# Attention and mixture of experts on one core: bias rows on TensorE, ScalarE bringing the projections out, router products a quarter into a tile, and one deviation ahead of two placings

## The reference

```
x = x + gnn(layernorm(x), adj)
x = x + ffn(layernorm(x))

gnn(n, adj):  h = n @ W.T + b_W
              e = leaky((h @ a1)[:, None] + (h @ a2)[None, :] + b_a)    # slope 0.2
              e = where(adj > 0, e, -9e15)
              return softmax(e, axis=1) @ h
ffn(n):       logits = n @ Wr + br;  the 2 best of 64 experts, gates = softmax of the 2
              out = sum over the 2 of gate * (relu(n @ W1[e] + b1[e]) @ W2[e] + b2[e])
```

## Time and profile before

| what | value |
|---|---|
| median of three runs | 280.89 us (279.63 to 281.43) |
| profiled execution, whole | 280.6 us |
| profiled execution, span | 278.9 us |
| mean granted TensorE clock | 0.918 |
| busy PE / DVE / ACT / POOL | 222.4 / 218.6 / 172.0 / 166.4 us |

### The profile page before, as it was taken

How to read it: one execution, slowest core, us unless ns; L and a number is a source line. 1 busy time by engine, 2 the same in 40 slices (tenths; PEclk the granted TensorE clock), 3 DMA queues, 4 the chain that set the end, 5 groups by cost and what they waited for, 6 DMA issues and landing times.

```text
span 278.9 us, 6179 instructions
## 1 busy us (share of the span) xinstructions
PE 222.4 (80%) x1849; PEld 212.8 (76%) x1849; DVE 218.6 (78%) x629; ACT 172.0 (62%) x386; POOL 166.4 (60%) x194
## 2 busy tenths in 40 slices
PE   1493399898968796886985368999999999999840
PEld 1372399798968696786984357999999999999740
DVE  4857989998999989999958733889887766766464
ACT  2743668797666585765751506878877777777400
POOL 5850011634478848888875755444888888866600
PEclk9999579999979999997998556999999999999995
DMA  6993454488474950810991113223148710100067
GB/s 162 227 199 71 79 94 79 82 211 209 139 185 89 285 179 12 292 32 19 374 418 49 59 43 91 66 57 80 42 133 321 256 41 31 40 28 24 31 199 262
DMA packets 11119, 36.88 MB, mean 132 GB/s; under 512 B 2256, under 2 KB 2832, under 8 KB 10320
## 3 DMA queue, kind: packets, MB, share of 16 engines
q0 software_dynamic: 5232, 14.98, 24.6%
q1 hardware_dynamic: 5424, 21.11, 21.6%
q10 hardware_dynamic: 432, 0.40, 0.5%
HBM read 39.36 MB, written 5.51 MB: 161 GB/s over the span
## 4 chain that ended last, share of the span: by engine, by line
PE 49%; DVE 27%; issue 9%; DMA 7%; POOL 5%; ACT 1%; SPq 1%; POOLq 0%; DVEq 0%; ACTq 0%
PE bank L1090 16%; PE bank L1102 15%; DVE arena L693 8%; PE bank L988 6%; DVE arena L699 4%; PE bank L972 4%; POOL table L419 2%; DVE arena L684 2%; DMA arena<-result 2%; DMA xs<-in_x 2%; PE bank L938 2%; DVE xs L705 2%; PE bank L1079 1%; PE bank L948 1%; DVE st L708 1%
## 5 line engine op out<-in xcount | busy, mean ns | idle before, releaser
L988 PE MATMUL bank<-arena 128*128 128x130 f32 x512 | 62.7, 279 | 1.4 <-ACT arena L542 1.3
L988 PEld LDWEIGHTS bank<-arena 128*128 128x128 f32 x512 | 60.3, 194 | 2.1 <-DVE xs L705 1.5
L1090 PE MATMUL bank<-arena 128*128 x384 | 60.4, 281 | 0.1
L1102 PE MATMUL bank<-w2s,arena 128*128 x384 | 58.8, 276 | 0.2 <-issue 0.2
L419 POOL DMA_INDIRECT table<-rows_in,pos x32 | 47.9, 1496 | 11.9 <-issue 8.1
L1090 PEld LDWEIGHTS bank<-arena 128*128 128x128 f32 x384 | 51.2, 194 | 0.5 <-issue 0.2
L1102 PEld LDWEIGHTS bank<-w2s,arena 128*128 128x128 f32 x384 | 50.6, 192 | 0.6 <-issue 0.6
L972 PE MATMUL bank<-ident,arena 128*128 128x128 f32 x256 | 35.5, 299 | 19.0 <-DVE arena L699 19.0
L868 DVE SCALAR_TENSOR_TENSOR arena<-bank,arena 128x128 f32 x96 | 33.6, 350 | 21.7 <-PE bank L1102 20.6
L972 PEld LDWEIGHTS bank<-ident,arena 128*128 128x128 f32 x256 | 32.5, 156 | 20.1 <-DVE arena L699 20.1
L601 ACT ACTIVATE arena<-bank,arena 128x128 f32<-128x128 f32 x96 | 35.1, 366 | 18.1 <-PE bank L1090 16.9
(11 more groups left out here) (190 smaller groups left out, 274.1 us busy)
## 6 DMA issues: line engine op xcount, KB each, us to landing
arena<-in_adj POOLq DMA_DIRECT2D x16, 512.0 KB, 5.4
w2s<-in_w SPq DMA_DIRECT2D x8, 768.0 KB, 4.6
arena<-in_w SPq DMA_DIRECT2D x6, 1024.0 KB, 9.2
arena<-in_w SPq DMA_DIRECT2D x4, 512.0 KB, 4.9
w2s<-in_w SPq DMA_DIRECT2D x4, 512.0 KB, 3.8
xs<-in_x SPq DMA_DIRECT2D x4, 256.0 KB, 6.3
arena<-result SPq DMA_DIRECT2D x2, 512.0 KB, 4.3
arena<-result SPq DMA_DIRECT2D x4, 256.0 KB, 6.1
```

The source lines that it names most:

```text
L988: ins = pe.matmul(OB[t % 2][:, 0:D + 2], pt_r[:, t % 2, j, :], h[:, j, :], start=(j == 0), stop=(j == T - 1))
L1090: ins = pe.matmul(hp(p, b), w1u[:, p % UW, P * b:P * b + P], xT_all[:, bass.ds(column, P)], start=True, stop=True)
L1102: ins = pe.matmul(yp(p), hT[:, p % UH, b, :], w2s[:, bass.ds(u, 1), b, :].rearrange("p e d -> p (e d)"), start=(b == 0), stop=(b == HB - 1))
```

## The change

On PE, the four quarters of the score row now come with only the turns of the quarters between them, and all projections behind them. Each projection is followed by a matmul of one row (a row of ones times the bias row `hbias`) into the same PSUM columns, which adds the bias. `xhT` lies in the second buffer of `pt_r`. The projections are brought out by ACT: two pairs of tiles and a quarter of s8 ahead of its scores of tile 0, the other six pairs and the rest of s8 ahead of its scores of tile 1. DVE, in place of ACT, writes the normalised rows of tiles 12 to 15; it sets eight small constants ahead of the statistics and no longer behind the projections. POOL loads blocks 2 and 3 of adj behind all four chunks of statistics. In attend, `route_b` stands behind 4 of the 16 products and no longer behind 8. At the end of attention, POOL makes the deviation of tiles 12 and 13 ahead of the two placings of tile 9, and DVE does place of group 3 ahead of the residual of tile 14.

```diff
-    PLACED = [..., (1, 7, 14), (2, 8, 15), (2, 9, 15)]
+    PLACED = [..., (1, 7, 14), (2, 8, 15)]
...
 # GpSimd
-                if c < 3:
-                    load(c + 1)
+                if c == 0:
+                    load(1)
+            load(2)
+            load(3)
...
             rstd_of(6)
+            place(2, 9)
             rstd_of(7)
...
 # ScalarE
             scale(2)
-            scale(3)
...
+            def h_evac(c):
+                act.wait_ge(s_h, c + 1)
+                act.activation(h[:, 2 * c:2 * c + 2, 0:D + 1],
+                               bank[4 + c % 4][:, 0:2 * (D + 1)].rearrange("p (t d) -> p t d", t=2), ACT.Copy).then_inc(s_hs, 1)
+
+            def slope(t0, t1):
+                act.wait_ge(s_hs, t1 // 2)
+                act.activation(s8[:, t0:t1], h[:, t0:t1, D], ACT.Copy, scale=1.0 - SLOPE).then_inc(s_s8, 1)
+
+            h_evac(0)
+            h_evac(1)
+            slope(0, 4)
+
             def scores(t):
-                if t == 0:
-                    act.wait_ge(s_s8, 1)
+                if t == 1:
+                    for c in range(2, 8):
+                        h_evac(c)
+                    slope(4, T)
+                if t in (0, 4):
+                    act.wait_ge(s_s8, 1 + t // 4)
...
 # VectorE
             xT_evac(0)
+            penalty(0)
+            dve.wait_ge(s_nm, 4)
+            for t in range(12, T):
+                ins = dve.tensor_scalar(xh[:, t, :], xs[:, t, :], rstd[:, t:t + 1], nm2[:, t:t + 1], ALU.mult, ALU.add)
+            ins.then_inc(s_norm3, 1)
             xT_evac(1)
-            penalty(0)
             xT_evac(2)
-            dve.wait_ge(s_was, 1)
-            h_evac(0)
-            h_evac(1)
             penalty(1)
-            for c in range(2, 6):
-                h_evac(c)
             scores(0)
-            h_evac(6)
-            h_evac(7)
-            dve.wait_ge(s_hs, 8)
-            dve.tensor_scalar(s8[:, :], h[:, :, D], 1.0 - SLOPE, None, ALU.mult).then_inc(s_s8, 1)
...
             leaky(T - 1)
+            place(3)
             residual(T - 2)
-            place(3)
             top2(4)
...
 # TensorE
-                        ins = pe.matmul(bank[4 + c % 4][:, j * (D + 1):(j + 1) * (D + 1)], xhT[:, P * t:P * t + P],
-                                        wt_s[:, :], start=True, stop=True)
+                        at = bank[4 + c % 4][:, j * (D + 1):(j + 1) * (D + 1)]
+                        pe.matmul(at, xhT[:, P * t:P * t + P], wt_s[:, :], start=True, stop=False)
+                        ins = pe.matmul(at, ones_f[0:1, :], hbias[0:1, :], start=False, stop=True)
...
-                        if j == T // 2 and t == LAST[q] + 2:
+                        if j == T // 4 and t == LAST[q] + 2:
                             route_b(q)
```

More of the change, by code:

```diff
@@ L25, in build @@
     LAST = [START[q + 1] - 1 for q in range(NG)]
-    PLACED = [(0, 0, 8), (0, 1, 9), (0, 2, 10), (0, 3, 11), (1, 4, 12), (1, 5, 13), (1, 6, 13), (1, 7, 14), (2, 8, 15), (2, 9, 15)]
+    PLACED = [(0, 0, 8), (0, 1, 9), (0, 2, 10), (0, 3, 11), (1, 4, 12), (1, 5, 13), (1, 6, 13), (1, 7, 14), (2, 8, 15)]
     LNS = [(t, t + 2) for t in range(0, T - 2, 2)] + [(T - 2, T - 1), (T - 1, T)]
@@ L102, in build @@
         zl = xT_all[:, 0:TOPK * T * D].rearrange("p (k t d) -> p k t d", k=TOPK, t=T)
-        xh, xhT = z_r[:, 1, :].rearrange("p (t d) -> p t d", t=T), z_r[:, 2, :]
+        xh, xhT = z_r[:, 1, :].rearrange("p (t d) -> p t d", t=T), pt_r[:, 1, :, :].rearrange("p t i -> p (t i)")
         s8 = sb("s8", [P, T])
@@ L207, in build @@
         s_norm = sem("s_norm")
+        s_norm3 = sem("s_norm3")
         s_xT = sem("s_xT")
@@ L650, in stats @@
                 dve.tensor_scalar(ve[:, 4 * c:4 * c + 4], mv[:, 4 * c:4 * c + 4, 1], EPS, None, ALU.add).then_inc(s_stat, 1)
[L652 to L658, removed]
             def xT_evac(b):
@@ L676, in _ @@
             dve.memset(padrow[:, :, :], 0.0).then_inc(s_set, 1)
+            dve.wait_ge(s_pool, 4)
+            dve.wait_ge(s_set, 1)
+            dve.tensor_scalar(sidx[0:P // 2, :], pidx[0:P // 2, :], 2.0, None, ALU.mult)
+            dve.tensor_scalar(sidx[P // 2:P, :], pidx[P // 2:P, :], 2.0, 1.0 - P, ALU.mult, ALU.add)
+            for into in (r_lo, r_hi, r_blk):
+                dve.tensor_copy(into[E:E + 1, :], iota_p[E:E + 1, 0:TAB])
+            for k in range(1 + TOPK):
+                ins = dve.tensor_scalar(padrow[:, k, ID_COL:ID_COL + 1], pidx[:, :], float(DUMP + (E + (k - 1) * P if k else 0)), None, ALU.add)
+            ins.then_inc(s_rows, 1)
             for c in range(4):
@@ L924, in turn_x @@
             def turn_x(b):
-                pe.wait_ge(s_norm, b + 1)
+                if b < 3:
+                    pe.wait_ge(s_norm, b + 1)
+                else:
+                    pe.wait_ge(s_norm3, 1)
                 for c in range(CB):
@@ L954, in _ @@
             pe.wait_ge(s_was, 1)
-            for b in range(4):
[L956 to L961, removed]
+            scores_row(0)
+            turn_x(2)
+            scores_row(1)
+            turn_x(3)
+            scores_row(2)
+            scores_row(3)
+            pe.wait_ge(s_set, 1)
+            for b in range(4):
+                project(b)
             def turn(t):
@@ L1033, in _ @@
             route_a(5)
+            route_c(4)
             route_b(5)
-            route_c(4)
             route_a(6)
```

## The result

The changed kernel takes **285.56 us** (median of four runs, 284.63 to 286.12) against 281.16 for the kernel before, 1.015 times as long (95% interval 1.009 to 1.022). The forecast was 273.4 us with a range up to 277.3: wrong in sign. (The kernel before, timed again beside the experiments, had medians of 279.9 to 280.6 us.) The profiled execution takes 286.12 us with a span of 284.3, 5.4 us more than the span before, of which the experts' stage behind the first fetch of rows makes 1.4 (115.3 us against 113.9; it lies between 113.9 and 115.6 in all runs here, also in the fastest). The other 4.0 us are 6.5 lost at the start, less 1.6 and 0.9 won behind it.

A forecast was written before the change was run, and what follows sets the result against it. The prediction took PE's chain to bound the start, DVE attention and POOL the placings behind it. Start 4.6, router 1.6 and placings 1.3 sum to 7.5 us: 280.9 - 7.5 = 273.4 us, range 271.8 to 277.3.

The forecast's parts named there:

- part three: ACT and PE at the start: each projection takes 0.22 us, its bias matmul another 0.22.
- rival (a): Projections at the start: bias matmuls don't overlap, about 0.16 us more per change of tile, 277.8 us; chance 0.11.
- the slower case (c): Projections at the start: changes of tile cost 0.27 us each, kernel slower than before at 282.0 us; chance 0.03.
- the bounds of the start: Start's gain of 4.6 us: 5.0 without DVE's wait, 3.9 if PE's clock falls while waiting 2 us for ACT.
- The start, part one: Twelve projections leave PE's stretch ahead of the last score-row quarter: first z at 20.6, gain 2.6 us.
- Part two: DVE's list at the start loses 1.74 us of work and a 0.69 us wait; leaky(2) could begin at 36.9.
- ScalarE's part: ACT brings out the projections at the start; DVE waits 0.4 to 0.5 us for low(1).
- Router: Router's products in attention come 0.9 us sooner, ending DVE's 0.79 us waits in groups 0 and 1: 1.6 us.
- Placings: POOL at the end of attention: the first of the eight last placings begins at 150.5, not 151.85, 1.3 us gained.
- The stretched deviation: POOL's deviation of tiles 12 and 13, beside DVE's leaky, takes 2.75 us instead of 0.73.
- Sum: Whole kernel: 4.6 + 1.6 + 1.3 = 7.5 us gained, median 273.4 us.

The follow-up runs named there:

- full height: The changed kernel with its 16 bias matmuls on tiles of 128 rows (identity times replicated bias rows): 274.36 us, 0.976 of the kernel before.
- the run with 64 rows: The changed kernel with bias matmuls on tiles of 64 rows (1/64 in each, times equal bias rows): 280.02 us in one run.
- the two runs with four changes: The changed kernel with four 258-column bias matmuls in a row ahead of eight projections: 278.23 us with one-row tiles, 276.2 with 128 rows.

## Why the prediction was wrong

**The step that failed** is in part three: "its bias matmul streams the same 129 columns, so I take another 0.22", with its rival (a) put at 0.11 and the slower case (c) at 0.03. The columns were right (0.22 in full height). The change of tile was 0.19 us each, 0.16 in (a); and what neither rival had is that the clock level falls under it. Together each change came to (20.2 - 7.1) / 32 = 0.41 us, above the 0.33 from which (c) made the kernel slower by over 1%; by (c)'s sum 0.41 gives 280.9 + 13.1 - 7.5 = 286.5 us, and 285.6 was measured. The only term for a falling clock was 0.7 us, in the bounds of the start, for a wait of 2 us; the fall cost 5.5. The place of (c) was right; its price for a change was reached only with the clock's share, about half of it, which (c) didn't name; and its chance was too small.

**Why I gave it so little.** I set the trace against the rule of the Trainium skill (TensorEngine Tiling (Array Packing), Key Properties) with one pair of merged rows, 64*1 and then 65*128, and read no gap between them. A merged row of eight hides its own spacing, and the ends of matmuls in it are modelled. The single records say otherwise. Timeline of PE of the kernel before, a window that holds the last four of the eight:

```profile
162.32 0.36 PE L1061 MATMUL bank<-r_slot,radix 64*1 64x24 f32 x4
162.61 0.53 PE L1066 MATMUL bank<-r_lo,side 65*128 65x96 f32 x1
```

Four records of 0.2 us each within 0.36 stand some 0.05 apart, so the last begins near 162.48, and L1066 0.13 later. A gap was there to be seen, though about 0.1 us long where the granted clock is 0.50, less than the 0.28 us that the same level shows further down; these matmuls have 24 columns, and the row couldn't have given the price. What the runs show agrees with the rule: each change of mode costs a pause, 0.19 us here. That it is the engine draining is the page's word for it; the rows show the distance between starts only.

**The start, part one:** the mechanism right; that it came out better, 3.7 us in place of 2.6 (3.2 in the run of full height), is luck as far as the traces show. PE comes up to its full pace at the start at another moment in each trace, though the code up to there is nearly the same. In the changed kernel's trace:

```profile
12.97 1.91 PE L947 MATMUL bank<-arena,x2T 128*128 128x512 f32 x2
...
15.53 1.03 PE L947 MATMUL bank<-arena,x2T 128*128 128x512 f32 x2
```

Here the pace had doubled by 15.5, where I had it stay at 18; over the twelve traces with this start it did so between 15.0 and 18.1, and the first z began between 19.27 and 20.72. The last of these is the run with 64 rows, where it doubled at 18: 0.1 us from the forecast's 20.6. That this is the clock level is taken from the pace alone; the column of the granted clock reads 1.00 from 12 to 20 us in both kernels, at the half pace too. **Part two:** right, shown with full height: third leaky at 36.97 against my 37.4, and 16.85 us behind the first z against my 16.8. **ScalarE's part:** right in the run of full height (0.50 us wait). **Router:** 1.6 forecast, 1.6 in the trace, 1.8 in the medians. **Placings:** 1.3 forecast, 0.9 in one trace and 0.8 between two, nothing in the medians; the idle 1.4 us of POOL ahead of 143.15 is its price, which my sum had. The stretched deviation took 2.75 us, as assumed. **Sum:** with only the failed step mended, 274.4 us against the forecast 273.4.

## What to carry to other kernels

Adding a bias by a matmul of one row is cheap in columns and dear in changes: give it the height of its neighbours (here the identity times the replicated row). Putting all of one height together saves the changes too, but where that makes TensorE wait it can cost as much: 278.2 us here. Where a rule of the Trainium skill speaks against an edit and only one merged row speaks for it, look at the single records before trusting the row. And when a cost on PE is put at its columns, ask what it does to the clock level: the same pauses cost 5.7 us with it high and 11.2 where it fell.

## What the hardware showed that I had not expected

- A change between a tile of 128 rows and one of 1, 32 or 64 rows costs 0.19 us at the high level and about 0.28 at the low one (0.727 less two times 0.223), each way, in the four kernels that alternate them.
- PE entered as busy without a break was at 0.50 of its clock: with bias tiles of one row from 22.4 us, with 32 rows from 24, with 64 and 128 rows not while the projections ran. A pause of 1.7 to 1.9 us was followed by the same fall in the two runs with four changes, one of 1.80 us in the run of full height by none. Why 64 rows keep the level with the same pauses stays open; no run here shows it.
- The column of the granted clock read 1.00 at the start of every trace looked at, while PE went at half its later pace (two records of 512 columns in 1.71 us at 12.97, in 0.87 at 15.53): there the distance between records is the better witness.
- A wide addition on GpSimd (four of 128x512) ran beside a DVE instruction that took 6.44 us in place of 2.29. Before, only the other direction was in my rows: a GpSimd step stretched by DVE.
